# A layer's late work inside a chunked recurrence: late normalisings reordered, VectorE's third step split around the output's normalising, late transposes and one inverse product placed later

## The chip, the cores and the metric

One core of a Trainium2 chip runs the whole program. The metric is the device time in microseconds (us) of one execution; the time shown for a kernel is the median of its runs.

## The reference

Input x has 8 sequences of 1024 tokens with 256 channels, all float32. Six residual blocks follow each other, each on the layer-normed x:

```
x = x + 0.5 * ffn0(LN(x))          # silu(gate) * up, 768 hidden, int weights / 127
x = x + gated_delta_attention(LN(x))  # 16 heads, key 64, value 128, causal conv of 4 taps
x = x + 0.5 * ffn0(LN(x))
x = x + 0.5 * ffn1(LN(x))          # token shift, sigmoid(r) * (relu(k)^2 @ Wv)
x = x + block_attention(LN(x))     # 16 heads of 16, blocks of 64 tokens, rope, softmax
x = x + 0.5 * ffn1(LN(x))
```

The gated delta attention is a recurrence over tokens with a state S of 64 x 128 per head: S = a_t (S - b_t k_t k_t' S) + k_t v_t', o_t = S' q_t, then an RMS norm of o and a product with Wo.

## The kernel before, in words

**Passes.** The tokens are taken in 16 groups of 512 (two per sequence). One pass of the loop handles one group: the first feed-forward block, the projections and convolutions, and then the recurrence in 8 chunks of 64 tokens, written with the inverse of a unit triangular 64 x 64 matrix per head. A pass takes about 450 us here. Everything behind the recurrence (the second half of the layer for the group before: `tail`) is cut into steps and put between the parts of the recurrence, as filler. After the 16th pass the last group's tail runs alone.

**Order by hand.** Every engine has its own instruction stream, and the order in it is written out. Each engine's `tail` is a Python generator; `fill(n)` advances it n times. Ten steps come ahead of chunk 0 (`FILL_FIRST`), then 24 slots (`SLOTS`), three per chunk: slots 3c, 3c+1 and 3c+2 in chunk c (`FILL`). The group's 512 tokens are worked on as two halves of 256, h = 0 and 1, each a stream of 20 late steps; `LATE_AT` says in which slot each step of each half stands. In what follows "step 4 of half 0" is index 4 of that list. The steps on TensorE are: 0 transposes of the normed half (`x{h}s`), 1 token shift products, 2 value product, 3 transposes for the attention (`x{h}a`), 4 query/key/value rows, 5 spread, 6 transposed queries and keys (`kt`), 7 to 10 scores, 10 to 13 weighted values, 14 transposes of the output, 15 output product, 16 transposes for the last feed-forward block (`x{h}u`), 18 shift products, 19 value product. Half 0 has step 2 in slot 2, step 3 in slot 4, and step s in slot s+1 from there on; half 1 has steps 0 and 1 in slots 3 and 4, and step s in slot s+4 from step 2 on.

**VectorE's part of a step** has two pieces, so its streams yield twice per step: in a slot all first pieces run, then all second ones. `values` (lines 602 to 612) adds to x and takes the statistics of the half (`stats`, 493 to 503); GpSimd raises the variance to the power -1/2 (`rstd`, 1092 to 1096); `normal` (505 to 511) waits for that and writes the normed half, for which TensorE's transposes wait (1664). `mix` (582 to 600) makes the two shifted inputs of the last block from ScalarE's copy of the transposes.

**A chunk c on TensorE** (2109 to 2170): wait for the state, product with the old state, slot 3c, transposes of the normalised output of chunk c-2 (two halves through one PSUM bank, bank 2, which ScalarE must copy out before it is written again: `copied`), query product, output of chunk c-1, `solve` (needs `right_side`, line 2032), the rest of the output, slot 3c+1, `new_state`, the projection of a finished part, keys transposed, slot 3c+2. **On VectorE** (978 to 1023): `right_side(c)`, slot 3c, `mean_square(c-1)`, slot 3c+1, `s_update(c)`, `keys(c+1)`, `normalise(c-1)` (934 to 939, it reads what GpSimd made of the mean square), slot 3c+2.

**The inverse in two halves.** GpSimd inverts 32 x 32 cells by substitution (`substitute`, 1169 to 1179), in pieces between its own slots: the second half's substitutions 8 to 15 stand between slots 1 and 2, 16 to 30 in chunk 1. SyncE moves the cells through DRAM, and TensorE and ScalarE make the corner blocks from them with two products: `inverse_q` and `inverse_t`. In chunk 3 the second half's `inverse_q(1,0)` waits for bank 2 (`copied`), then for the cells (`d_back`, 2135 and 2136), and stands ahead of `solve`; `inverse_q(1,1)` stands behind slot 10, `inverse_t` in slot 11 and chunk 4 (waits at 2120 and 2131). ScalarE's copies for them (1450 to 1463) stand in its own stream, some behind an exponential of the softmax (1340 to 1345).

**PSUM ring.** Tail steps use banks 5 to 7 in turn, in the order of `tail_ring`; a step that claims a bank waits (1658) until the step three names ahead of it is read out. The wait instruction that the profile names is the last of several in a row.

## Time and profile before

| What | Value |
| --- | --- |
| Median of 3 runs | 7401.95 us (7399.27 to 7410.97) |
| The profiled execution, its own time | 7407.52 us |
| Its span (first to last instruction) | 7405.7 us, mean granted TensorE clock 0.925 |
| TensorE busy | 85% |
| VectorE, ScalarE, GpSimd busy | 62%, 35%, 31% |
| DMA | mean 31 GB/s, 10.2% of 16 engines |

Times in the timelines are from the start of the span. The pass looked at below is the fifth; its recurrence starts near 2073 us, and the next pass starts near 2286 us. "PEq L2032" as the releaser of a wait of PE means that PE's own sequencer stood at the waiting instruction of line 2032. A row of a timeline may merge instructions; x32 of 64x128 float32 matmuls are 16 matmuls of the source, as float32 goes through the array twice.

### The profile page before, as it was taken

Reading aid. Unit: us, or ns where it says so; the run is one execution under the profiler, and the core shown is the slowest. Engines: PE = TensorE matmul, PEld = TensorE weight load, DVE = VectorE, ACT = ScalarE, POOL = GpSimd, SP = SyncE. Lnnn points to the kernel's source line nnn. Section 1 sums busy time; section 2 is a strip of 40 time slices with the busy share of each in tenths; the row PEclk is TensorE's granted clock in tenths of the full one; section 3 lists DMA queues with packets and bytes.
Section 4 is the critical chain, followed back from the end, with each engine's and each line's share of the span. In section 5 each row is a group of like instructions: output and inputs, shape, how many; then the busy total and the mean of one; then the engine's idle time right before and its main releaser. Section 6 shows DMA issues by size and latency. Waiting matters only on the chain. (4 is left out here: it accounts for less than half of the span.)

```text
span 7405.7 us, 162691 instructions
## 1 busy us (share of the span) xinstructions
PE 6273.3 (85%) x60192; PEld 4534.7 (61%) x60192; DVE 4571.7 (62%) x9685; ACT 2619.0 (35%) x5275; POOL 2269.1 (31%) x3893
## 2 busy tenths in 40 slices
PE   7888888888888888888888889888888888888887
PEld 4665656656576665756656566565756657566575
DVE  6656575565756657566566656657566575665664
ACT  3324243332423325243242433425233252433421
POOL 2513224141331514315133241413315143151421
PEclk9999998999989999999999989899999999999998
DMA  1111001011010101001110010110101110011100
GB/s 53 33 38 22 27 31 39 30 23 40 21 36 30 33 35 29 23 29 33 41 23 27 31 39 30 23 40 21 36 30 33 39 25 23 29 33 41 23 27 5
DMA packets 376536, 226.37 MB, mean 31 GB/s; under 512 B 336896, under 2 KB 353920, under 8 KB 367488
## 3 DMA queue, kind: packets, MB, share of 16 engines
q1 hardware_dynamic: 375680, 215.29, 10.2%
q8 instruction: 496, 8.13, 0.5%
q14 instruction: 360, 2.95, 0.1%
HBM read 156.54 MB, written 58.72 MB: 29 GB/s over the span
## 5 line engine op out<-in xcount | busy, mean ns | idle before, releaser
L833 DVE SCALAR_TENSOR_TENSOR PS<-BIG,CW,PS 128x512 f32<-128x512 f32 x1536 | 1155.2, 753 | 210.2 <-DVEq L831 132.0
L1586 PE MATMUL PS<-BIG 64*64 64x128 f32 (+3 forms) x23200 | 1067.6, 255 | 203.7 <-PEq L2032 105.8
L1586 PEld LDWEIGHTS PS<-BIG 64*64 64x64 f32 (+2 forms) x23200 | 906.7, 134 | 344.8 <-issue 332.9
L1586 PE MATMUL PS<-XT,BIG 128*128 128x512 f32 x2048 | 1058.8, 650 | 51.3 <-PEq L1897 51.3
L1589 PE MATMUL PS<-CST,BIG 128*128 128x128 f32 x3536 | 560.0, 297 | 314.5 <-PEq L1664 82.7
L1589 PEld LDWEIGHTS PS<-CST,BIG 128*128 128x128 f32 x3536 | 416.6, 150 | 434.6 <-issue 417.8
L1249 POOL TENSOR_TENSOR FR<-MS,NHALF 128x8 f32<-128x8 f32 x128 | 209.9, 1640 | 1477.3 <-POOLq L1248 1303.5
L1586 PEld LDWEIGHTS PS<-XT,BIG 128*128 128x128 f32 x2048 | 398.5, 206 | 395.6 <-issue 386.2
L1095 POOL TENSOR_TENSOR RSTD<-VAR,NHALF 128x2 f32<-128x2 f32 x202 | 142.3, 704 | 1574.9 <-POOLq L1094 1568.2
L1586 PE MATMUL PS<-BIG,CST 128*128 128x256 f32 (+1 forms) x1360 | 505.0, 516 | 112.9 <-PEq L1967 98.9
L1177 POOL TENSOR_TENSOR BIG<-BIG 128x30 f32<-128x30 f32 (+14 forms) x960 | 499.9, 521 | 136.5
L1174 POOL TENSOR_TENSOR BIG<-BIG 128x30 f32<-128x30 f32 (+14 forms) x960 | 474.7, 494 | 139.8 <-POOLq L1213 12.0
L1586 PE MATMUL PS<-XT,WG 128*128 128x256 f32 (+1 forms) x1200 | 433.2, 487 | 45.0 <-PEq L1658 20.7
L1586 PE MATMUL PS<-BIG,VO 128*128 128x256 f32 x2080 | 468.3, 382 | 0.9 <-PEq L2216 0.9
L1586 PEld LDWEIGHTS PS<-BIG,CST 128*128 128x128 f32 x1360 | 264.2, 206 | 330.5 <-issue 305.1
L1586 PEld LDWEIGHTS PS<-CST,BIG 64*64 64x64 f32 (+1 forms) x4224 | 328.4, 166 | 191.7 <-issue 189.1
L1586 PEld LDWEIGHTS PS<-BIG,VO 128*128 128x128 f32 x2080 | 394.4, 191 | 66.4 <-issue 14.4
L1586 PE MATMUL PS<-XT,WU 128*128 128x256 f32 (+1 forms) x1200 | 406.5, 462 | 1.0 <-issue 1.0
L964 DVE TENSOR_REDUCE MS<-BIG 128x4 f32<-128x512 f32 x256 | 174.4, 685 | 364.4 <-DVEq L963 364.0
L1421 ACT ACTIVATE BIG<-PS 128x512 f32<-128x512 f32 x512 | 304.2, 594 | 206.4 <-ACTq L1420 206.3
L1586 PE MATMUL PS<-WD,BIG 128*128 128x256 f32 x1584 | 352.5, 381 | 21.9 <-PEq L1632 18.3
L1586 PE MATMUL PS<-CST,BIG 64*64 64x64 f32 (+1 forms) x4224 | 334.1, 235 | 31.9 <-PEq L1864 22.9
(152 smaller groups left out, 10183.3 us busy)
## 6 DMA issues: line engine op xcount, KB each, us to landing
BIG<-in_wv SPq DMA_DIRECT2D x16, 2048.0 KB, 7.5
BIG<-in_wo SPq DMA_DIRECT2D x16, 2048.0 KB, 8.7
BIG<-in_wq SPq DMA_DIRECT2D x16, 1024.0 KB, 4.8
BIG<-in_wk SPq DMA_DIRECT2D x16, 1024.0 KB, 7.3
cells_in<-BIG SPq DMA_DIRECT2D x128, 128.0 KB, 2.7
BIG<-cells_in SPq DMA_DIRECT2D x32, 512.0 KB, 3.8
cells_out<-BIG SPq DMA_DIRECT2D x32, 512.0 KB, 2.6
cells_nat<-BIG SPq DMA_DIRECT2D x32, 512.0 KB, 3.1
```

Of the source, the lines that this page charges most:

```text
L833: op = v.scalar_tensor_tensor(y, pre[:, j:j + G], CW[:, i * TAPS + j:i * TAPS + j + 1], y, ALU.mult, ALU.add)
L964: v.tensor_reduce(MS[:, 4 * x:4 * x + 4], v3(SQO[c][:, 512 * x:512 * x + 512], 4), AX, ALU.add)
L1095: q.tensor_tensor(out=RSTD[:, 2 * k:2 * k + 2], in0=VAR[:, 2 * k:2 * k + 2], in1=NHALF[:, 0:2], op=ALU.pow).then_inc(rstd_ready, 1)
L1174: q.tensor_tensor(out=tmp, in0=each(cells[:, 0:j, j], j, w), in1=over(cells[:, j, j + 1:SUB], j, w), op=ALU.mult)
L1177: q.tensor_tensor(out=cells[:, 0:j, j + 1:SUB], in0=cells[:, 0:j, j + 1:SUB], in1=tmp, op=ALU.add)
L1249: q.tensor_tensor(out=FR[:, :], in0=MS[:, :], in1=NHALF[:, :], op=ALU.pow).then_inc(fr_ready, 1)
L1421: a.activation(TH[:, (i % 2) * G:(i % 2) * G + G], conv_bank(i), ACT.Tanh, scale=0.5).then_inc(cth_ready, 1)
L1586: return nc.tensor.matmul(out_, l, r, start=start, stop=stop)
L1589: return nc.tensor.matmul(out_, in_, ident, is_transpose=True, start=True, stop=True)
```

## The change

- In VectorE's tail each slot now yields once more, behind the first piece of half 0. `fill(2)` is then a whole slot; in slots 3c+2 with c below 7 there is `fill(1)`, `normalise(c-1)`, `fill(1)`: half 0's first piece stands ahead of the normalising, the rest behind it.
- `normal(1)` of slot 2 is put ahead of `values(0)` of that slot (it stood behind it). `normal(0)`, which stood at the end of slot 2, is put into slot 3, behind `mix(1)`.
- The transposes `x{h}u` (TensorE, with ScalarE's copy) move from step 16 to step 17: half 0 from slot 17 to 18, half 1 from slot 20 to 21. VectorE's `mix(h, 1)` moves with them. The ring's order is changed to match.
- In chunk 3, `inverse_q(1,0)` and ScalarE's copy for it move from ahead of `solve(3)` to behind the output of chunk 2, just ahead of slot 10; the wait for the cells and for bank 2 moves with it, and the wait for the copy (`qp_ready`) now stands behind slot 10.

```diff
--- before.py
+++ after.py
@@ -50,7 +50,7 @@
     names.update({5: [f"vd{h}0", f"vd{h}1"], 6: [f"kt{h}0", f"kt{h}1"], 7: [f"sc{h}0"], 8: [f"sc{h}1"]})
     for i in range(5):
         names[9 + i] = ([f"av{h}{i - 1}"] if i else []) + ([f"pt{h}{i}"] if i < 4 else []) + ([f"sc{h}{i + 2}"] if i < 2 else [])
-    names.update({14: [f"oa{h}"], 15: [f"ao{h}"], 16: [f"x{h}u"], 18: [f"k{h}u", f"r{h}u"], 19: [f"v{h}u"]})
+    names.update({14: [f"oa{h}"], 15: [f"ao{h}"], 17: [f"x{h}u"], 18: [f"k{h}u", f"r{h}u"], 19: [f"v{h}u"]})
     return names
 
 
@@ -679,7 +679,8 @@
                     yield
                     values(h, 0)
                     yield
-                    normal(h, x, TXN, txn_ready)
+                    if h == 1:
+                        normal(h, x, TXN, txn_ready)
                     yield
                     yield
                     yield
@@ -730,9 +731,9 @@
                     yield
                     normal(h, x, TXN, txn_ready)
                     yield
+                    yield
+                    yield
                     mix(h, 1)
-                    yield
-                    yield
                     yield
                     yield
                     yield
@@ -758,18 +759,23 @@
                 yield
                 streams = late(0), late(1)
                 for n in range(SLOTS):
-                    now = [streams[h] for h in range(2) if n in LATE_AT[h]]
-                    for s in now:
-                        next(s)
+                    if n == 2:
+                        normal(1, x, TXN, txn_ready)
+                    for h in range(2):
+                        if n in LATE_AT[h]:
+                            next(streams[h])
+                        if h == 0:
+                            yield
                     if n == 0:
                         hidden(1, 4)
                         hidden(1, 5)
                     if n == 1:
                         down(1)
-                    if n == 2:
-                        normal(1, x, TXN, txn_ready)
-                    for s in now:
-                        next(s)
+                    if n == 3:
+                        normal(0, x, TXN, txn_ready)
+                    for h in range(2):
+                        if n in LATE_AT[h]:
+                            next(streams[h])
                     yield
 
             def cp(i):
@@ -987,12 +993,12 @@
                 for c in range(CHUNKS):
                     right_side(c, 0)
                     right_side(c, 1)
-                    fill(FILL[c][0])
+                    fill(2)
                     if c >= 1:
                         mean_square(c - 1)
                     if c == CHUNKS - 1:
                         dve.drain().then_inc(r_free, 1)
-                    fill(FILL[c][1])
+                    fill(2)
                     if c == CHUNKS - 1:
                         break
                     s_update(c, 0)
@@ -1000,10 +1006,11 @@
                     if c >= 5:
                         projected(c - 5, XS[p])
                     keys(c + 1)
+                    fill(1)
                     if c >= 1:
                         normalise(c - 1, 0)
                         normalise(c - 1, 1)
-                    fill(FILL[c][2])
+                    fill(1)
                 last = CHUNKS - 1
                 s_update(last, 0)
                 s_update(last, 1)
@@ -1012,7 +1019,7 @@
                 projected(last - 5, XS[p])
                 input_stats()
                 mean_square(last)
-                fill(FILL[last][2])
+                fill(2)
                 input_normal()
                 xt_copy()
                 normalise(last, 0)
@@ -1392,8 +1399,8 @@
                     act.drain().then_inc(oat_ready, 1)
                     yield
                     yield
+                    yield
                     transposed(f"x{h}u")
-                    yield
                     yield
                     squared(h, 1)
                     yield
@@ -1495,8 +1502,6 @@
                         act.drain().then_inc(a_done, 1)
                     if c >= 2:
                         output(c - 2, 0)
-                    if c == 3:
-                        inverse_q(0, bank(2))
                     for x in range(2):
                         act.wait_ge(u_ps, 1)
                         act.sem_inc(u_ps, -1)
@@ -1507,6 +1512,8 @@
                         output(c - 2, 1)
                     if c >= 1:
                         square_out(c - 1, 1)
+                    if c == 3:
+                        inverse_q(0, bank(2))
                     fill(FILL[c][1])
                     if c == 3:
                         inverse_q(1, bank(2))
@@ -1823,8 +1830,8 @@
                     pe.sem_inc(oat_ready, -1)
                     rows(f"ao{h}", OT, WOUT, KT, ao_ps)
                     yield
+                    yield
                     transposed(f"x{h}u")
-                    yield
                     yield
                     shift(h, 1)
                     yield
@@ -2130,27 +2137,24 @@
                         pe.wait_ge(ti_ready, 1)
                         pe.sem_inc(ti_ready, -1)
                         output_t(c - 2, 0)
+                    solve(c, 0)
+                    solve(c, 1)
+                    if c >= 2:
+                        copied()
+                        output_t(c - 2, 1)
+                    if c >= 1:
+                        output(c - 1, 1)
+                    if c == CHUNKS - 1:
+                        break
                     if c == 3:
                         copied()
                         pe.wait_ge(d_back, 96)
                         pe.sem_inc(d_back, -96)
                         inverse_q(1, 0, bank(2))
-                    solve(c, 0)
-                    solve(c, 1)
-                    if c >= 2:
-                        if c == 3:
-                            pe.wait_ge(qp_ready, 1)
-                            pe.sem_inc(qp_ready, -1)
-                        else:
-                            copied()
-                        output_t(c - 2, 1)
-                    if c >= 1:
-                        output(c - 1, 1)
-                    if c == CHUNKS - 1:
-                        break
                     fill(FILL[c][1])
                     if c == 3:
-                        copied()
+                        pe.wait_ge(qp_ready, 1)
+                        pe.sem_inc(qp_ready, -1)
                         inverse_q(1, 1, bank(2))
                     new_state(c)
                     if c in (2, 4):
```

## Rows read from the trace of the kernel before

**Rows 1.** The page of the kernel before: busy time and share of each engine.

```profile
PE 6273.3 (85%) x60192; PEld 4534.7 (61%) x60192; DVE 4571.7 (62%) x9685; ACT 2619.0 (35%) x5275; POOL 2269.1 (31%) x3893
```

**Rows 2.** Waits of TensorE (PE): whose line, us in total, times, longest.

```profile
PE PS L1586 <- PEq L2032: 105.8, 32, 5.9
...
PE PS L1586 <- PEq L1717: 95.5, 43, 4.4
PE PS L1589 <- PEq L1664: 82.7, 38, 4.4
...
PE PS L1586 <- PEq L2160: 35.2, 16, 2.2
...
PE PS L1586 <- PEq L2136: 31.6, 16, 2.1
```

**Rows 3.** Timeline of TensorE, chunks 0 and 1: start, us, instructions, [idle before].

```profile
2093.37 1.10 PE L1586 MATMUL PS<-S,KQ 64*64 64x128 f32 x32 [0.29 <-PEq L2112]
2098.16 1.09 PE L1589 MATMUL PS<-CST,BIG 128*128 128x128 f32 x4 [3.68 <-PEq L1664]
...
2107.67 5.39 PE L1586 MATMUL PS<-BIG 64*64 64x128 f32 x48 [4.81 <-PEq L2032]
2112.98 0.69 PE L1589 MATMUL PS<-CST,BIG 128*128 128x128 f32 x4
```

**Rows 4.** Timeline of VectorE (DVE), chunks 0 to 2.

```profile
2093.75 0.68 DVE L606 SCALAR_TENSOR_TENSOR BIG<-BIG,PS 128x512 f32<-128x512 f32 x1
...
2096.59 1.43 DVE L510 TENSOR_SCALAR BIG<-XB,MVR,RSTD 128x256 f32<-128x256 f32 x2
2105.12 1.36 DVE L510 TENSOR_SCALAR BIG<-XB,MVR,RSTD 128x256 f32<-128x256 f32 x2 [7.11 <-DVEq L508]
2106.41 2.15 DVE L928 SCALAR_TENSOR_TENSOR BIG<-PS,NBG,VO 128x128 f32<-128x128 f32 x8
...
2134.52 0.73 DVE L510 TENSOR_SCALAR BIG<-XB,MVR,RSTD 128x256 f32<-128x256 f32 x2 [1.04 <-DVEq L508]
```

**Rows 5.** Timeline of GpSimd (POOL), chunks 1 and 2.

```profile
2104.26 0.71 POOL L1095 TENSOR_TENSOR RSTD<-VAR,NHALF 128x2 f32<-128x2 f32 x1 [0.24 <-POOLq L1094]
...
2129.02 2.51 POOL L1105 TENSOR_TENSOR BIG<-BIG 128x512 f32<-128x512 f32 x2 [0.28 <-POOLq L1103]
```

**Rows 6.** Timeline of TensorE, chunks 2 and 3.

```profile
2135.08 2.03 PE L1586 MATMUL PS<-CST,BIG 64*64 64x64 f32 x64
...
2154.72 3.09 PE L1586 MATMUL PS<-BIG 32*32 32x32 f32 x96 [2.14 <-PEq L2136]
...
2159.35 0.66 PE L1589 MATMUL PS<-CST,BIG 128*128 128x128 f32 x4
```

**Rows 7.** Timeline of ScalarE (ACT), chunk 3.

```profile
2153.66 0.60 ACT L1476 ACTIVATE VO<-PS 128x512 f32<-128x512 f32 x1 [0.20 <-ACTq L1474]
```

**Rows 8.** Timeline of SyncE's queue, the last issue of the second scatter.

```profile
2133.60 1.21 SPq L434 DMA_DIRECT2D BIG<-cells_nat  x2
```

**Rows 9.** DMA issues by kind: KB each, median us to landing.

```profile
BIG<-cells_nat SPq DMA_DIRECT2D x64, 128.0 KB, 3.7
```

**Rows 10.** Timeline of VectorE, chunks 3 and 5.

```profile
2173.40 0.69 DVE L644 TENSOR_TENSOR BIG<-PS,CST 128x512 f32<-128x512 f32 x1 [1.87 <-DVEq L643]
...
2229.66 1.28 DVE L938 TENSOR_TENSOR BIG<-PS,FR 128x512 f32<-128x512 f32 x2
...
2233.51 0.28 DVE L668 TENSOR_TENSOR BIG<-PS,NBR 128x128 f32<-128x128 f32 x1
```

**Rows 11.** Timeline of TensorE, chunks 6 and 7.

```profile
2233.99 1.07 PE L1589 MATMUL PS<-CST,BIG 128*128 128x128 f32 x8 [2.88 <-PEq L1816]
...
2263.22 2.12 PE L1586 MATMUL PS<-BIG 64*64 64x128 f32 x32 [1.30 <-PEq L2032]
```

**Rows 12.** Busy time by stretch: PE, PEld, DVE, ACT, POOL, granted clock, DMA.

```profile
2113.00:2152.00 39.00, 38.66 (x504) 29.94 (x504) 29.11 (x72) 10.00 (x17) 23.52 (x35) 1.00 0.21 49
2165.00:2176.00 11.00, 8.65 (x140) 6.15 (x140) 6.47 (x16) 2.74 (x6) 2.34 (x4) 0.69 0.01 2
```

More of the change, by code:

```diff
@@ L732, in late @@
                     yield
-                    mix(h, 1)
                     yield
                     yield
+                    mix(h, 1)
                     yield
```

## The prediction

> **What bounds the kernel now.** I read the page first: TensorE is busy 85% of the span and no other engine is near it [rows 1], so time is won where TensorE stands still, or where its order makes it stand still later. TensorE's waits come next [rows 2]. I looked where they lie in the timelines of several passes: except for the first and last microseconds they come in the same places, with nearly the same length, in all 16 passes, so I work one pass out (the fifth) and multiply by 16. The stretch that the change touches is the recurrence, some 210 of 450 us.
>
> In chunk 1 TensorE waits 3.68 us for normed rows (line 1664) and then 4.81 us for the right side (line 2032) [rows 3]. VectorE shows why: it has finished `normal(1)` late, at 2098.02, and then waits 7.11 us at `normal(0)` before it may start `right_side(1)` at 2106.41 [rows 4]. That wait ends with GpSimd's `rstd(0)` at 2104.26 [rows 5], which stands in GpSimd's queue behind eight substitutions. A small operation of the filler holds up the recurrence through VectorE's in-order queue.
>
> **The parts, one by one.** The unit is one pass; "lead" is how far TensorE is ahead of the trace before.
>
> *Slots 2 and 3.* `normal(1)` now runs at 2093.75 for 1.43 us and `values(0)` with its statistics, 2096.59 - 2093.75 = 2.84 us, behind it [rows 4]. The transposes of slot 3 can start at about 2095.3 instead of 2098.16 [rows 3]. `right_side(1)` starts at about 2098.0 instead of 2106.41, and `solve` follows 1.26 us later (2107.67 - 2106.41) if TensorE is there; it is at about 2100, since the 4.7 us of work between the two waits was done at a low clock. Lead: about 8 us. What is late next is `normal(0)`: VectorE reaches it after `right_side(1)` (2.15 us) and `mix(1)` by about 2104, and must still wait for `rstd(0)`, done at 2104.97; with its 1.36 us it ends at 2106.4, and the transposes of slot 4 start there instead of at 2112.98 [rows 3 to 5]. Lead: 6.5 us; about 3 us if the new 4.6 us wait brings half clock for as long as in this stretch.
>
> That lead is not kept. GpSimd's chain of substitutions does not move (it never waited in this stretch for what gets earlier), so the rope additions behind it still end at 2129.02 + 2.51 = 2131.5 [rows 5]. TensorE's `kt` in slot 7 needs them and starts at 2135.08 now [rows 6]: lead at most 3.5 us. Behind them in GpSimd's queue are `rstd(1)`, the power for the output's norm and the masked keys; passing through `normal(1)`, which already waits 1.04 us [rows 4], they cost about another 1. **I take 2.5 us.** Bounds: 0, if that chain does not move at all; 6.5, if it does not bind.
>
> *`inverse_q(1,0)`.* The wait before it (2136) is named for the cells, but the cells are long there: the last transfer is issued by 2133.60 + 1.21, and such a transfer lands 3.7 us after its issue, at about 2138.5 [rows 8, 9]. What ends the wait at 2154.72 [rows 6] is bank 2: ScalarE's copy of the transposed output runs 2153.66 to 2154.26 [rows 7], behind an exponential that needs VectorE's softmax piece. In the new place `solve`, 4 transposes and the output's second part cover that copy: 32 + 16 matmuls took 5.39 us at half clock, so some 2.7 us at full, and the transposes 0.7 us [rows 3], and the product waits instead for the next copy of bank 2, about 0.9 us, as ScalarE has four passes of 0.6 us [rows 7] to do behind `solve`. So 1.97 us (31.6 / 16 [rows 2]) minus 0.9 and a little for lost overlap: slot 10 starts about 1.6 us earlier. Since the output of chunk 2 is then ready over 3 us earlier, `mean_square(2)`, the softmax piece and ScalarE's second `inverse_q` copy come earlier too, and the 2.20 us wait at 2160 (35.2 / 16) gives back another 0.5. **I take 2.1 us.** Bounds: 0 and 1.97 + 2.20 = 4.2.
>
> *Third step on both sides.* `normalise` takes 1.28 us for both halves [rows 10]. In slot 5 and slot 8 its place changes nothing: the rest of the slot waits for TensorE either way. In slot 11 it did lie in a hole: VectorE did it and then still waited 1.87 us for scores at 2173.40 [rows 10]. Now scaling and the softmax of half 0 come first and the normalising delays half 1's softmax, the exponential and ScalarE's `inverse_t` copy behind it, for which TensorE already waits at 2120: **a loss of 1.0 us** (bounds 0 and 1.28). In slot 14 it is the other way: TensorE waits 4.4 us at scores for a ring bank that `scaled(0,3)` frees (line 1717 [rows 2]; the longest of that row), and that small operation stood behind the normalising. **Gain 1.2 us** (0 to 1.28).
>
> *Transposes one step later.* In slot 17 VectorE does the normalising, then `mix(0,1)`, and only then `scaled(1,3)` at 2233.51 [rows 10], for which TensorE waits 2.88 us until 2233.99 [rows 11]. `mix`, all that lies between the normalising's end at 2230.94 and 2233.51, so 2.6 us, is now in slot 18, where `mean_square` waits for TensorE anyway. **Gain 2.6 us** (0 to 2.88). In slot 20 `mix(1,1)` goes too, but there the normalising now stands behind `values(0,1)`, ends near 2260.8, and chunk 7's transposes of the output need it: TensorE's 1.30 us at `solve` [rows 11] turn into a wait of the same size a little ahead of it. **0 us** (0 to 1.3). The moved transposes and copies are the same instructions; no DMA moves.
>
> *The cost of company.* VectorE's pieces that now run while GpSimd substitutes are slower: `normal` took 1.43 and 1.36 us there and 0.73 us elsewhere [rows 4]. My sum has the long values. The Trainium skill (SBUF — State Buffer, section "SBUF: two separate sides") says that VectorE in a two-port mode, or with two SBUF inputs, and GpSimd lock each other out for a whole instruction. By it more of VectorE's work in slots 2 and 3 would come out slower, but only ahead of `rstd(0)`, where VectorE waits anyway.
>
> Sum: 2.5 + 2.1 - 1.0 + 1.2 + 2.6 = 7.4 us a pass, 16 passes: 118 us. The tail that runs alone at the end has waits of the same kind; I take nothing for it, within 4 us either way. Against the profiled execution: 7407.5 - 118 = 7289; that execution is 5.6 us above the median of the runs, so the median to expect is 7284 us, 1.6% less.
>
> **The rivals.**
>
> *GpSimd keeps all of the first part.* Its chain runs from `rstd(1)` through 24 substitutions to the masked keys with hardly a gap. If it also sets the scores of slot 8, the 2.5 us are gone and 4.9 us a pass stay: 7402 - 78 = 7324. For it: the lead shrinks at every station of that chain. Against: TensorE, not GpSimd, had the last word at `kt` (3.5 us spare). Chance 0.15.
>
> *More comes than I count.* Half clock follows the waits: 0.69 granted in the stretch around 2170 [rows 12]. If shorter waits keep the clock up there and the losses in slot 11 hide, 10 to 11 us a pass: about 7235. Chance 0.12.
>
> *Slower: the clock in chunks 1 to 3.* From 2113 to 2152 TensorE runs at full clock and is busy 38.66 of 39 us [rows 12]. The change puts new short waits into just this stretch (`kt`, scores of slot 8, bank 2) and brings two products of tiny matmuls closer together. At half clock a microsecond of work takes two. If more than 7.4 us of full-clock work in a pass runs at half clock that does not now, the kernel is slower; with 10 us of it, 16 x 2.6 = 42 us slower, 7444. Against: each of the new waits in it is 1 us or less, and TensorE stays busy between them. Chance 0.06.
>
> *It doesn't do what it says.* `normal(0)` still waits for the same power, only one slot later; if every lead is taken back by the next in-order wait, in slots 4, 11 and 21, nothing is left: 7395 to 7402. Chance 0.05.
>
> **How the numbers follow.** My forecast has 0.62. The range 7225 to 7345 leaves out the last two rivals and little else: its lower end is 11 us a pass, its upper end 3.6 us. About 0.2%, 15 us, is what a measurement of this kernel can tell from no change. Faster 0.88 (forecast, the first two rivals, most of the fringe), same 0.05, slower 0.07.
>
> **What would show it.** Right: the 7.11 us wait of VectorE ahead of `right_side(1)` is gone, and a wait of about 1 us stands ahead of `normal(0)` in slot 3; TensorE waits near 4.6 us at line 1664 in slot 4; `kt` starts just behind the rope additions; the waits at d_back and at `scaled(1,3)` are gone; the wait at `inverse_t` grows by about 1 us. Passes last about 443 us. Wrong: the clock below 1.0 between `kt` and slot 9; the wait at 2160 grown; passes at 450.

## The result and the profile after

The changed kernel takes 7283.84 us (median of 4 runs, 7280.8 to 7293.09), the kernel before 7406.46 us: ratio 0.9827 (95% interval 0.9811 to 0.9843). The prediction was 7284 us. So the forecast held, and since a sum can be right with wrong terms, most of what follows is on its terms.

The page of the changed kernel: the span is 125 us shorter. Some 86 us of that are waits of TensorE. The other 39 us are its busy time, for the same 60192 matmuls [rows 1]: it stood 1005 us of this trace at half clock (1.2 GHz granted and not 2.4), and 1115 us of the trace before. The busy times of the other engines are within 10 us of what they were.

```profile
span 7280.3 us, 162691 instructions
...
PE 6234.2 (86%) x60192; PEld 4502.9 (62%) x60192; DVE 4575.7 (63%) x9685; ACT 2616.4 (36%) x5275; POOL 2260.1 (31%) x3893
```

Waits of TensorE, as in [rows 2]. Line 2039 is the old 2032 (right side), 1724 the old 1717 (scores), 1671 the old 1664 (normed rows), 2164 the old 2160 (`qp_ready` behind `new_state`), 2152 the old 2136 (cells and bank 2).

```profile
PE PS L1596 <- PEq L1671: 120.8, 55, 5.5
...
PE PS L1593 <- PEq L1724: 102.6, 68, 3.2
...
PE PS L1593 <- PEq L2164: 30.9, 16, 1.9
...
PE PS L1593 <- PEq L2039: 22.1, 17, 1.4
...
PE PS L1593 <- PEq L2152: 6.6, 16, 0.5
...
PE PS L1596 <- PEq L1823: 3.5, 16, 0.2
```

The wait at the right side fell from 105.8 to 22.1 us, the one ahead of the moved inverse product from 31.6 to 6.6, and `scaled(1,3)` now costs 3.5 us in all (it was 2.88 us in each pass). The wait for normed rows grew from 82.7 to 120.8 us: that is where the stall of chunk 1 went.

Chunks 0 and 1 of the fifth pass. TensorE, VectorE and GpSimd, as in [rows 3 to 5]; this pass starts its recurrence 33.5 us earlier than in the trace before, so 2107.67 there answers to 2074.1 here:

```profile
2065.25 3.00 PE L1593 MATMUL PS<-BIG 64*64 64x128 f32 x48 [1.37 <-PEq L2039]
2073.78 1.09 PE L1596 MATMUL PS<-CST,BIG 128*128 128x128 f32 x4 [5.53 <-PEq L1671]
...
2098.96 2.08 PE L1593 MATMUL PS<-CST,BIG 64*64 64x64 f32 x64 [1.55 <-PEq L1665]
```

```profile
2060.23 0.98 DVE L510 TENSOR_SCALAR BIG<-XB,MVR,RSTD 128x256 f32<-128x256 f32 x2
...
2061.90 0.69 DVE L608 SCALAR_TENSOR_TENSOR XB<-BIG,XB 128x512 f32<-128x512 f32 x1
...
2063.98 2.16 DVE L934 SCALAR_TENSOR_TENSOR BIG<-PS,NBG,VO 128x128 f32<-128x128 f32 x8
...
2072.27 1.36 DVE L510 TENSOR_SCALAR BIG<-XB,MVR,RSTD 128x256 f32<-128x256 f32 x2 [2.39 <-DVEq L508]
```

```profile
2061.91 1.14 POOL L1184 TENSOR_TENSOR BIG<-BIG 128x210 f32<-128x210 f32 x1
...
2066.19 1.08 POOL L1181 TENSOR_TENSOR BIG<-BIG 128x234 f32<-128x234 f32 x1
...
2071.41 0.70 POOL L1102 TENSOR_TENSOR RSTD<-VAR,NHALF 128x2 f32<-128x2 f32 x1 [0.24 <-POOLq L1101]
...
2096.17 2.49 POOL L1112 TENSOR_TENSOR BIG<-BIG 128x512 f32<-128x512 f32 x2 [0.28 <-POOLq L1110]
```

`right_side(1)` starts at 2063.98, 8.9 us earlier in the pass. VectorE reaches `normal(0)` and waits 2.39 us for the power that GpSimd finishes at 2072.1, and the transposes of slot 4 wait 5.53 us for it. `kt` (2098.96) starts when GpSimd's rope additions are done (2096.17 + 2.49); in all 16 passes it starts 0.30 us behind their end.

Chunk 3, as in [rows 6, 7]: the moved product waits 0.49 us for bank 2, behind ScalarE's copy at 2119.75.

```profile
2118.57 0.66 PE L1596 MATMUL PS<-CST,BIG 128*128 128x128 f32 x4
2119.16 1.09 PE L1593 MATMUL PS<-BIG 64*64 64x128 f32 x16
2120.74 1.20 PE L1593 MATMUL PS<-BIG 32*32 32x32 f32 x64 [0.49 <-PEq L2152]
...
2129.51 0.68 PE L1593 MATMUL PS<-CST,KQ 64*64 64x64 f32 x16 [1.90 <-PEq L2164]
```

```profile
2119.27 0.59 ACT L1489 ACTIVATE BIG<-PS 128x512 f32<-128x512 f32 x1
2119.75 0.60 ACT L1483 ACTIVATE VO<-PS 128x512 f32<-128x512 f32 x1
```

To see each part of the sum I took, in every trace, the start of one VectorE operation per chunk, counted from the first `keys` operation of its pass, and the median over the 16 passes (us; for "pass", over 15; the last column is the lead; the names are those of VectorE's functions):

```
mark                before   changed   lead
right_side(1)        33.54     24.62   8.92
s_update(1)          45.01     41.75   3.26
right_side(3)        75.08     73.00   2.08
keys(4)              96.34     92.16   4.18
right_side(4)       106.31    103.48   2.83
right_side(5)       136.28    131.81   4.47
keys(6)             155.92    151.07   4.84
s_update(6)         177.17    168.97   8.20
s_update(7)         196.63    188.30   8.33
pass                449.10    441.18   7.92
```

Medians don't add exactly, and in chunks 3 to 5 a mark carries up to 1 us of noise: `right_side(5)` stands at 136.3 us in the kernel before and at 137.2 us in the one below that changes only slots 17 to 21. On the mean the 15 steps from one pass to the next give 8.2 us each, 123 of the 125 us.

### The profile page after: what moved, and what is told of

Same layout as the page of the kernel before. It is cut to its first block and busy times, and to the rows that moved or that the text cites. A ratio compares the mean times of both kernels' runs of the same rounds, so it can differ in the third digit from the quotient of the medians.

```text
span 7280.3 us, 162691 instructions
## 1 busy us (share of the span) xinstructions
PE 6234.2 (86%) x60192; PEld 4502.9 (62%) x60192; DVE 4575.7 (63%) x9685; ACT 2616.4 (36%) x5275; POOL 2260.1 (31%) x3893
## 5 line engine op out<-in xcount | busy, mean ns | idle before, releaser
L1593 PE MATMUL PS<-BIG 64*64 64x128 f32 (+3 forms) x23200 | 1011.0, 249 | 104.9 <-PEq L2127 36.9
L1593 PEld LDWEIGHTS PS<-BIG 64*64 64x64 f32 (+2 forms) x23200 | 854.6, 130 | 243.8 <-issue 231.9
L1596 PE MATMUL PS<-CST,BIG 128*128 128x128 f32 x3536 | 573.7, 302 | 321.5 <-PEq L1671 120.8
L1315 ACT ACTIVATE XT<-PS 128x512 f32<-128x512 f32 x136 | 82.1, 604 | 805.6 <-ACTq L1314 805.5
```

The lines of the kernel that those rows point to most:

```text
L1315: a.activation(XTH[:, :, h, 1:HG + 1], v3(ps, KT), ACT.Copy).then_inc(free, 1)
L1593: return nc.tensor.matmul(out_, l, r, start=start, stop=stop)
L1596: return nc.tensor.matmul(out_, in_, ident, is_transpose=True, start=True, stop=True)
```

## The experiments

Two theories stood against each other for every part: mine by its sum, and that the part does nothing or the opposite.

**The four parts alone**, each put into the kernel before. The tail's additional `yield` in each slot is in all of them and changes no order by itself; only the third kernel puts something at it.

The order of the normalisings:

```diff
@@ tail of VectorE, the steps, then the slots @@
-                    normal(h, x, TXN, txn_ready)
+                    if h == 1:
+                        normal(h, x, TXN, txn_ready)
...
+                    if n == 2:
+                        normal(1, x, TXN, txn_ready)
                     for h in range(2):
                         if n in LATE_AT[h]:
                             next(streams[h])
...
-                    if n == 2:
-                        normal(1, x, TXN, txn_ready)
+                    if n == 3:
+                        normal(0, x, TXN, txn_ready)
                     for h in range(2):
                         if n in LATE_AT[h]:
                             next(streams[h])
```

> The kernel before with the new order of normal(0) and normal(1) alone. Theory A (the lead of chunk 1 is cut by GpSimd's rope additions, and some of it is kept): 2.1 to 2.5 us a pass are kept at right_side(3), so 34 to 40 us, 7366 us, ratio 0.995; right_side(1) 8 to 9 us earlier, TensorE's wait ahead of the transposes of slot 4 about 5 us. Rival (GpSimd's chain keeps all of it): ratio 1.000. Second rival (nothing binds when ScalarE and bank 2 are left as they were): over 5 us a pass, ratio 0.989.

Measured: 7378.05 us, ratio 0.996 (0.9946 to 0.9974). `right_side(1)` 8.9 us earlier, `s_update(1)` 3.2 us, `right_side(3)` 2.3 us, and `s_update(7)`, near the end of the pass, 1.7 us. TensorE's wait ahead of slot 4's transposes is 5.55 us. A lead of 8.9 us shrinks to a quarter, as in theory A; the ratios of both rivals (1.000 and 0.989) lie outside the interval.

The inverse product:

```diff
@@ TensorE @@
-                    if c == 3:
-                        copied()
-                        pe.wait_ge(d_back, 96)
-                        pe.sem_inc(d_back, -96)
-                        inverse_q(1, 0, bank(2))
                     solve(c, 0)
...
-                    fill(FILL[c][1])
                     if c == 3:
                         copied()
+                        pe.wait_ge(d_back, 96)
+                        pe.sem_inc(d_back, -96)
+                        inverse_q(1, 0, bank(2))
+                    fill(FILL[c][1])
+                    if c == 3:
+                        pe.wait_ge(qp_ready, 1)
+                        pe.sem_inc(qp_ready, -1)
                         inverse_q(1, 1, bank(2))
@@ ScalarE @@
-                    if c == 3:
-                        inverse_q(0, bank(2))
                     for x in range(2):
...
                         square_out(c - 1, 1)
+                    if c == 3:
+                        inverse_q(0, bank(2))
```

> The kernel before with inverse_q(1,0) and its copy moved alone. Theory A (the wait named for the cells is bank 2): the wait of 1.97 us shrinks to 0.5 to 0.9 us and keys(4) comes 2.0 us earlier after right_side(3), 30 to 35 us in all, ratio 0.9955. Rival (the cells are really late): the wait stays as long as the solve lets it, under 1 us a pass, ratio 0.998 to 1.000.

Measured: 7375.28 us, ratio 0.9949 (0.9933 to 0.9966). TensorE in chunk 3 of its sixth pass:

```profile
2580.63 0.63 PE L1592 MATMUL PS<-CST,BIG 128*128 128x128 f32 x4
2581.18 1.09 PE L1589 MATMUL PS<-BIG 64*64 64x128 f32 x16
2582.74 1.20 PE L1589 MATMUL PS<-BIG 32*32 32x32 f32 x64 [0.46 <-PEq L2148]
```

The wait of 1.97 us is 0.46 us, and `keys(4)` comes 2.7 us earlier than in the kernel before. The product itself starts some 1.8 us later in the pass than it did, so this kernel alone can't tell bank 2 from cells that land late. It could have been read off the trace before, where the cells had landed some 14 us before the wait began, that the name of the wait was not its cause. Two other kernels show it: with the normalisings alone the cells land as before (at 65.6 us of the pass, before 65.1) and the product, in its old place, starts 2.3 us earlier; and in the kernel with GpSimd's new order, further down, the cells land 7.3 us later than in the changed kernel, and the moved product starts at 77.4 us of the pass, before the change at 81.2.

The third step on both sides:

```diff
@@ recurrence of VectorE, end of chunk c @@
                     keys(c + 1)
+                    fill(1)
                     if c >= 1:
                         normalise(c - 1, 0)
                         normalise(c - 1, 1)
-                    fill(FILL[c][2])
+                    fill(1)
```

> The kernel before with VectorE's third step on both sides of normalise alone. Theory A (one slot loses what another gains): right_side(4) 1.0 to 1.3 us later, right_side(5) 1.2 to 1.4 us earlier against it, sum 0 within 0.5 us a pass, ratio 0.999 to 1.001. Rival (the split is a gain by itself, as it was in slot 14): 1.2 us a pass, ratio 0.9975.

Measured: 7468.36 us, ratio 1.0076 (1.0059 to 1.0093). Both theories missed: alone, this part makes the kernel 0.8% slower. The marks say where: `right_side(4)` 1.4 us later and `right_side(5)` 1.8 us earlier against it, as expected, and then `s_update(6)` 2.1 us and `s_update(7)` 3.3 us later than before. In slots 17 and 20 `mix` is still there. The split puts it ahead of the normalising in slot 17, and in slot 20 it puts the normalising behind `values(0,1)`, so that others get both late. VectorE in slot 17 of the sixth pass, and TensorE there and in chunk 7:

```profile
2695.06 0.17 DVE L588 COPY XT<-PREV 128x2 f32<-128x2 f32 x1 [0.65 <-DVEq L584]
...
2696.14 1.67 DVE L598 SCALAR_TENSOR_TENSOR BIG<-BIG,MU,XT 128x256 f32<-128x256 f32 x4
2697.73 1.28 DVE L941 TENSOR_TENSOR BIG<-PS,FR 128x512 f32<-128x512 f32 x2
2698.93 0.28 DVE L668 TENSOR_TENSOR BIG<-PS,NBR 128x128 f32<-128x128 f32 x1
```

```profile
2699.40 1.94 PE L1593 MATMUL PS<-CST,BIG 128*128 128x128 f32 x8 [3.62 <-PEq L1820]
...
2728.69 0.63 PE L1593 MATMUL PS<-CST,BIG 128*128 128x128 f32 x4 [1.51 <-PEq L2085]
...
2732.15 2.12 PE L1590 MATMUL PS<-BIG 64*64 64x128 f32 x32 [0.94 <-PEq L2036]
```

`mix` waits 0.65 us for its copy, which the normalising had covered, and `scaled(1,3)` comes behind both: TensorE waits 3.62 us, not 2.88. In chunk 7 it waits 1.51 us for the normalised output and then 0.94 us for the right side, where it had one wait of 1.30 us.

The late transposes and `mix`:

```diff
@@ VectorE @@
                     yield
-                    mix(h, 1)
                     yield
                     yield
+                    mix(h, 1)
                     yield
@@ ScalarE, and the same on TensorE @@
                     yield
-                    transposed(f"x{h}u")
                     yield
+                    transposed(f"x{h}u")
                     yield
```

> The kernel before with the late transposes and mix one step later alone. Theory A (mix stood ahead of scaled(1,3) and of right_side(7)): slot 17 gives 2.6 to 3.4 us and, as normalise stays ahead of values in slot 20, that slot gives another 1.3 us: 3.9 to 4.7 us a pass, 62 to 75 us, ratio 0.991. Rival (slot 20 gives nothing, as in the changed kernel): 2.6 to 3.4 us a pass, ratio 0.9935.

Measured: 7328.41 us, ratio 0.9892 (0.9873 to 0.9911), 83 us and the largest part. Slot 17's wait is 0.22 us, `right_side(7)` starts 5.6 us earlier. The interval holds theory A's 0.991 and not the rival's 0.9935; the gain is a little above A's 62 to 75 us. Slot 20 does give its part here: from `s_update(6)` to `s_update(7)` this kernel takes 17.8 us, the one before 19.5 us.

**The last two together**, as their effects alone were of opposite sign:

```diff
                     keys(c + 1)
+                    fill(1)
...
-                    mix(h, 1)
                     yield
                     yield
+                    mix(h, 1)
```

> The kernel before with two parts together: the third step on both sides of normalise, and the late transposes and mix one step later. Alone they gave 1.0076 and 0.9892. Theory A (what the split costs alone in slots 17 and 20 is mix, which it leaves behind the normalising there, so it costs little once mix is gone): ratio 0.989 to 0.991. Rival (the effects add): ratio 0.997.

Measured: 7360.25 us, ratio 0.9925 (0.9908 to 0.9941). Nearer to theory A, though beyond its 0.991, and clear of the 0.997 of plain addition. Against the late step alone the split costs some 0.3%, though the two intervals just touch (0.9911 and 0.9908). Over the ratios of the parts, -0.0040 (normals), -0.0051 (inverse) and -0.0075 (these two) make -0.0166, and the whole change measured -0.0173: apart from the pair, the parts add.

**What cuts the first lead.** Two edits of GpSimd's order in the changed kernel. First, its power for `normal(0)` moved between the substitutions:

```diff
@@ recurrence of GpSimd @@
                     fill(FILL[c][1])
-                    if c < 2:
-                        substitute(8 + 15 * c, 16 + 15 * c)
+                    if c == 0:
+                        substitute(8, 12)
                     if c == 1:
+                        substitute(23, 31)
                         finish_cells()
                     fill(FILL[c][2])
+                    if c == 0:
+                        substitute(12, 16)
```

> The changed kernel with GpSimd's rstd(0) of slot 2 put between substitutions 11 and 12 instead of behind 15. Theory A (what cuts the lead is the end of GpSimd's whole chain at the rope additions): the wait ahead of the transposes of slot 4 falls from 5.5 to 3 us or less, but right_side(3) comes at the same 73.0 us of the pass within 0.5 us, ratio to before 0.982 to 0.984. Rival (the wait in slot 4 and the clock behind it set the lead): right_side(3) 2 to 3 us earlier, ratio 0.977.

Measured: 7304.82 us, ratio 0.9858 (0.9831 to 0.9884). That is some 20 us above the changed kernel, but the two intervals overlap (0.9811 to 0.9843 there), so the times alone don't show it slower; the marks go against both theories: `right_side(3)` comes at 74.4 us of the pass, 1.4 us later than in the changed kernel. TensorE, VectorE and GpSimd around `kt` in its sixth pass:

```profile
2549.33 3.58 PE L1596 MATMUL PS<-CST,BIG 64*64 64x64 f32 x64 [3.78 <-PEq L1668]
```

```profile
2549.84 0.73 DVE L510 TENSOR_SCALAR BIG<-XB,MVR,RSTD 128x256 f32<-128x256 f32 x2 [6.94 <-DVEq L508]
```

```profile
2546.55 2.48 POOL L1112 TENSOR_TENSOR BIG<-BIG 128x512 f32<-128x512 f32 x2 [0.28 <-POOLq L1110]
2548.98 0.71 POOL L1102 TENSOR_TENSOR RSTD<-VAR,NHALF 128x2 f32<-128x2 f32 x1
```

The last of these stretches, by busy time and granted clock (columns as in [rows 12]), and below it the same 64 matmuls in the changed kernel:

```profile
2549.30:2552.80 3.50, 3.47 (x64) 3.41 (x64) 2.09 (x5) 0.60 (x1) 1.01 (x2) 0.53 1.20 188
```

```profile
2098.90:2101.00 2.10, 2.04 (x65) 2.00 (x65) 1.53 (x4) 0.60 (x1) 0.42 (x1) 1.00 0.94 149
```

`s_update(1)` came 2.7 us earlier still. But the rope additions end where they ended, TensorE waits 3.78 us at `kt` instead of 1.55, and the granted clock is 0.53 behind it, the level of 1.2 GHz, where the changed kernel has 1.00: the 64 matmuls take 3.58 us and not 2.08. From `right_side(2)` to `s_update(3)` the changed kernel has no half clock in any of its 16 passes, this one has a stretch in 14 (the kernel before in 4, of 3.4 us each). In those 14 passes TensorE had waited 3.4 to 5.1 us at `kt`; in the other two it had waited 2.4 and 2.5 us, and the 64 matmuls took 2.08 us. In the changed kernel the longest of these waits is 1.55 us, and in 12 of the 16 passes it is 0.86 us or less. `s_update(2)` is 1.7 us later than in the changed kernel. Arriving earlier at a fixed gate cost time.

Second, the rope additions ahead of the last four substitutions as well:

```diff
@@ recurrence of GpSimd, with the edit above @@
                     if c == 1:
-                        substitute(23, 31)
-                        finish_cells()
+                        substitute(23, 27)
                     fill(FILL[c][2])
...
+                    if c == 1:
+                        substitute(27, 31)
+                        finish_cells()
```

> The changed kernel with GpSimd's rstd(0) put between substitutions 11 and 12, and its rope additions of slot 5 ahead of the last four substitutions. Theory A (GpSimd's chain is what cuts the lead): kt of slot 7 starts 3 us or more earlier, right_side(3) 2.5 to 4 us earlier than in the changed kernel, ratio to before 0.974 to 0.977. Rival (the lead is then lost at the next station, masked keys or the cells of the second half, which now come 2.5 us later): ratio 0.981 or more.

Measured: 7295.94 us, ratio 0.9835 (0.9803 to 0.9868): the rival, though at a station that it didn't name. `kt` starts 3.7 us earlier in its pass than in the changed kernel (median), `right_side(3)` 0.4 us later, and between them the next transposes wait 3.25 us for `normal(1)`, whose power is now the operation behind the cells' copy:

```profile
2529.25 2.03 PE L1598 MATMUL PS<-CST,BIG 64*64 64x64 f32 x64
2534.54 0.63 PE L1601 MATMUL PS<-CST,BIG 128*128 128x128 f32 x4 [3.25 <-PEq L1676]
```

```profile
2530.58 1.94 POOL L1190 COPY BIG<-BIG 128x1024 f32<-128x1024 f32 x1 [0.17 <-issue]
2532.80 0.71 POOL L1102 TENSOR_TENSOR RSTD<-VAR,NHALF 128x2 f32<-128x2 f32 x1 [0.28 <-POOLq L1101]
```

So the gate is not one operation: each small one behind the substitutions is a gate of its own. All of them moved ahead, and the cells' end some 7 us later in the pass:

```diff
@@ recurrence of GpSimd, on top of the two edits above @@
                         substitute(1 + 15 * c, 8 + 15 * c)
+                    if c == 2:
+                        substitute(28, 31)
...
                     if c == 1:
-                        substitute(23, 27)
+                        substitute(23, 26)
+                    if c == 2:
+                        finish_cells()
                     fill(FILL[c][2])
...
                     if c == 1:
-                        substitute(27, 31)
-                        finish_cells()
+                        substitute(26, 28)
```

> The changed kernel with GpSimd's small late operations of slots 2, 5, 6 and 7 (two powers, the rope additions, the power for the output and the first masked keys) all put ahead of substitutions and of the cells' copy, which end some 7 us later in the pass. Theory A (the lead of chunk 1 is lost at the end of GpSimd's chain, station after station, and the cells have about 13 us to spare): right_side(3) 3 to 4 us earlier than in the changed kernel (69 to 70 us of the pass), kt near 56 us and no wait over 1 us behind it, ratio to before 0.973 to 0.976. Rival (the lead is lost to ScalarE and bank 2 in chunk 3, or the cells are now late): right_side(3) early, but keys(4) no more than 1 us earlier than 92.2 us, ratio 0.980 or more.

Measured: 7224.16 us, ratio 0.9753 (0.9733 to 0.9774). The changed kernel ran again beside it:

> The changed kernel as it is, beside the two below on the same chip. Both theories: ratio to the kernel before 0.981 to 0.984, passes of 441 us.

Measured: 7278.53 us, ratio 0.9828 (0.9808 to 0.9848). In the kernel with GpSimd's new order `right_side(3)` comes at 69.3 us of the pass, in this one at 73.1, and `keys(4)` at 88.3 and 92.3: the lead passes through chunk 3 whole. Theory A, in size too.

**What the split costs in the changed kernel.** Without it:

```diff
@@ recurrence of VectorE, changed kernel @@
                     keys(c + 1)
-                    fill(1)
                     if c >= 1:
                         normalise(c - 1, 0)
                         normalise(c - 1, 1)
-                    fill(1)
+                    fill(2)
```

> The changed kernel with normalise again ahead of the whole third slot. Theory A (the split gives 1.2 to 1.6 us in slot 14 and takes 1.3 us in slot 11 and 1.2 to 1.4 us in slot 20): 1.0 to 1.4 us a pass faster than the changed kernel, 16 to 22 us, ratio to the kernel before 0.980. Rival (the split carries part of the change's gain): slower than the changed kernel, ratio 0.985 or more.

Measured: 7250.25 us, ratio 0.977 (0.974 to 0.9799). With the split left out in chunks 3 and 6 alone:

```diff
-                    fill(1)
+                    if c not in (3, 6):
+                        fill(1)
                     if c >= 1:
                         normalise(c - 1, 0)
                         normalise(c - 1, 1)
-                    fill(1)
+                    fill(2 if c in (3, 6) else 1)
```

> The changed kernel with normalise ahead of the whole third slot in chunks 3 and 6 alone. Theory A: both losses of the split go and slot 14's gain stays: 2.6 us a pass faster than the changed kernel, 40 us, ratio to before 0.977. Rival (TensorE is held at the same places by others, as ScalarE's copies and the masked keys): under 1 us a pass, ratio 0.981 or more.

Measured: 7244.48 us, ratio 0.9773 (0.9746 to 0.98). Both beat the changed kernel; they can't be told apart by their times. The second gains what was expected (40 us; 34 to 39 against the two medians of the changed kernel), the first more than its 16 to 22 us (28 to 34). By the marks, without any split `right_side(4)` is 1.1 us earlier than in the changed kernel and `right_side(5)` 1.6 us later; with the split in place in slot 14 both are earlier, 1.3 and 0.8 us, and `s_update(7)` is 1.95 us earlier.

**Both together**, the best kernel of the study:

```diff
+                    if c not in (3, 6):
+                        fill(1)
...
-                        substitute(8 + 15 * c, 16 + 15 * c)
+                        substitute(8, 12)
...
+                        substitute(28, 31)
```

> The same, with normalise ahead of the whole third slot in chunks 3 and 6 too. Theory A: the two gains lie in different chunks and add: 5.5 to 6.5 us a pass faster than the changed kernel, ratio to before 0.968 to 0.971. Rival (they don't add, as the passes are held elsewhere): no faster than the kernel with the chunks' change alone, 0.976 or more.

Measured: 7171.75 us, ratio 0.9688 (0.9663 to 0.9713). TensorE and GpSimd in chunks 1 and 2 of its sixth pass (the first `keys` of this pass stands at 2448.23):

```profile
2504.07 2.03 PE L1602 MATMUL PS<-CST,BIG 64*64 64x64 f32 x64
2506.03 0.66 PE L1605 MATMUL PS<-CST,BIG 128*128 128x128 f32 x4
```

```profile
2497.30 2.51 POOL L1113 TENSOR_TENSOR BIG<-BIG 128x512 f32<-128x512 f32 x2 [0.24 <-POOLq L1111]
...
2502.59 0.71 POOL L1103 TENSOR_TENSOR RSTD<-VAR,NHALF 128x2 f32<-128x2 f32 x1 [0.24 <-POOLq L1102]
...
2506.22 1.65 POOL L1259 TENSOR_TENSOR FR<-MS,NHALF 128x8 f32<-128x8 f32 x1 [0.45 <-POOLq L1258]
2507.84 2.34 POOL L1122 TENSOR_TENSOR BIG<-BIG,CST 128x256 f32<-128x256 f32 x4
...
2510.44 1.96 POOL L1191 COPY BIG<-BIG 128x1024 f32<-128x1024 f32 x1 [0.17 <-issue]
```

`kt` (2504.07) and the transposes behind it start without a wait: the rope additions are done at 2499.8 and the power for `normal(1)` at 2503.3. The cells' copy (2510.44) is now the last of the group. GpSimd's order brings 54 us (7278.53 - 7224.16, the kernel without the two chunks' edit), and the two chunks 52 us on top of it (7224.16 - 7171.75), more than the 34 to 39 us that they bring in the changed kernel. Together that is 6.7 us a pass, where 5.5 to 6.5 were expected.

## Why the prediction was right, and where not

- **What bounds, and the sum.** Right: TensorE's share stayed and its waits shrank. 7.9 us a pass were gained where 7.4 were summed, and that it is so near is in part luck: slots 2 and 3 and slot 11 came out 0.75 us worse than their terms, slots 14 and 17 some 1.2 us better. The sum is one of waits, but 39 of the 125 us are busy time, that is clock. Most of that lies in chunks 0 and 1, where the gate at `kt` turns it into waiting again; in slot 17 it counts. There the passes aren't alike either: the clock fell in 9 passes of the kernel before and not in 7.
- **Slots 2 and 3, 2.5 us.** Measured: 2.1 at `right_side(3)` in the changed kernel, 2.3 alone. Its course was right, and its sizes partly: the wait ahead of slot 4's transposes is 5.53 us where I had 4.6, and half clock followed (the transposes took 1.09 us; the same at full clock take 0.66). VectorE's wait ahead of `normal(0)` was 2.39 us where about 1 us was said. `normal(0)` ended at 2073.6, which is 2107.1 in the time of the trace before; I had 2106.4. I had taken GpSimd's chain as fixed, and this power came 0.66 us later in every pass. Of the sizes behind it two were wrong and cancelled. The 3.5 us that TensorE had to spare at `kt` were read in the fifth pass, where they are 3.55; over the 16 passes of that trace they are 2.3 to 3.9 with a median of 2.7, and as `kt` starts 0.3 us behind the additions, the lead there is 2.4 us. The further loss up to `right_side(3)` was 0.3 us and not about 1. That GpSimd's chain takes the lead back was a statement of the trace's order alone; the kernels that move its small operations show it, and show that it holds at three stations one behind the other: the power for `normal(0)`, the rope additions, the power for `normal(1)`.
- **The inverse product, 2.1 us.** Measured: from 2.08 to 4.18 us of lead, 2.1. The wait for bank 2 ahead of it was 0.49 us, not 0.9, and the one at the old line 2160 gave back 0.3 us (35.2 to 30.9 us in 16 passes), not 0.5.
- **Slot 11, a loss of 1.0 us.** Measured: 4.18 to 2.83, 1.35 us. Right in its course on VectorE, where `normalise` (2138.78) now stands between two softmax pieces and all of its 1.28 us falls on the path. Wrong in where TensorE would feel it: the wait at `inverse_t` was to grow by about 1 us and did not (line 2127, the old 2120: 36.9 us, before 37.4); a new wait of 1.99 us stands ahead of it, at the scores (line 1724), which claim a ring bank. VectorE and TensorE in the changed kernel:

```profile
2131.89 0.29 DVE L668 TENSOR_TENSOR BIG<-PS,NBR 128x128 f32<-128x128 f32 x1
2134.84 0.69 DVE L644 TENSOR_TENSOR BIG<-PS,CST 128x512 f32<-128x512 f32 x1 [2.66 <-DVEq L643]
...
2138.78 1.29 DVE L944 TENSOR_TENSOR BIG<-PS,FR 128x512 f32<-128x512 f32 x2 [0.19 <-DVEq L943]
2139.99 0.68 DVE L644 TENSOR_TENSOR BIG<-PS,CST 128x512 f32<-128x512 f32 x1
```

```profile
2140.96 1.42 PE L1593 MATMUL PS<-KQ,BIG 64*64 64x256 f32 x8 [1.99 <-PEq L1724]
...
2144.49 1.92 PE L1593 MATMUL PS<-BIG 32*32 32x32 f32 x64 [2.11 <-PEq L2127]
```

- **Slot 14, 1.2 us.** Measured: 2.83 to 4.47, 1.6 us. TensorE's wait at the scores fell from 4.37 to 3.18 us, by 1.2. From `s_update(4)` to `right_side(5)` every kernel without the split in slot 14 takes 10.12 to 10.15 us (means over 16 passes), and every kernel with it 8.6 to 8.8, so the split gives 1.3 to 1.5 us there; why more than the wait is not settled, and the last tenths of the 1.6 are within the noise of the mark.
- **Slot 17, 2.6 us.** The wait gave 2.66 us (2.88 to 0.22). The mark behind it, `s_update(6)`, is 3.4 us further ahead than `keys(6)`, and the rest is clock: between the two the 7 passes of the kernel before without half clock take 20.55 us and the 9 that have some (3.4 us of it in most) take 22.2, while all 16 of the changed kernel take 17.89 with none. 20.55 - 17.89 is the wait, and in 9 of 16 passes some 1.6 us more come with it. This is the term that was most too small: the wait was priced right, and the clock behind it at nothing.
- **Slot 20, 0 us.** Right, as worked out: a wait for the normalised output of 1.36 us takes the place of the 1.30 us at `solve`.

```profile
2219.03 0.63 PE L1596 MATMUL PS<-CST,BIG 128*128 128x128 f32 x4 [1.36 <-PEq L2088]
```

The step that failed on its reasons is the part on the split as a whole. I had it at plus 0.2 us in sum, gain and loss in two slots, and it costs: 0.8% alone, 0.3% with `mix` out of the way, and the changed kernel is faster without it. Slots 17 and 20 were costed with both edits in place, so that the split's loss in slot 20 was hidden in the zero there: from `s_update(6)` to `s_update(7)` the kernel before takes 19.5 us, the late step alone 17.8 us, and the changed kernel 19.3 us, so the split costs 1.5 us there. The slower rival, the clock in chunks 1 to 3, did not come: the clock stayed at full in the changed kernel between `kt` and slot 9. It did come in the kernel that moved one power alone. The rival that more would come, by the clock, was right in kind and wrong in place: from `keys(4)` to `right_side(4)`, the stretch it named, both traces have 75 us of half clock in 16 passes, and what went away was in chunks 0 and 1, in 4 passes of chunk 3, and in slot 17. Of the rival on GpSimd, the part that was true is inside the 2.5 us.

What stays open: why slot 14 gave more than its wait, and which of several small differences makes the clock fall in some passes and not in others behind the same wait of 2.88 us.

## What to carry to other kernels

A stall that is taken away moves its engine up to the next gate, and with in-order queues that gate is often one queue's whole chain: walk the lead from station to station before you count it, and if several small operations stand behind long ones, move all of them or none. Cost an edit once alone and once with the others: here one of four parts was a loss that its neighbours hid. Look at the clock behind a wait as well as at the wait. The name of a wait is that of the last instruction in the queue, so check when each thing it waits for was there.

## What the runs showed of the hardware

- Arriving earlier at a gate that doesn't move can cost time. With a wait of 3.78 us ahead of them, the 64 matmuls of `kt` took 3.58 us (granted clock 0.53), and 2.08 us behind a wait of 1.55 us (granted clock 1.00). In the kernel that moved one power the clock is at half behind this wait in 14 passes of 16.
- VectorE and GpSimd slow each other both ways. `normal` beside the substitutions took 0.98 and 1.36 us in the changed kernel against 0.73 us elsewhere [rows 4]. The substitution at 2061.91 took 1.14 us; it started just behind VectorE's addition to x at 2061.90 (two inputs in SBUF, 0.69 us), and the same substitution in the kernel before, which met the statistics instead, took 0.58. So it lost 0.56 us, where the other's operation had 0.68 us to run. The Trainium skill (SBUF — State Buffer, section "SBUF: two separate sides") has it as a lock, between a VectorE operation with two inputs in SBUF and a GpSimd operation that reads SBUF, that the first to start holds for its whole instruction. This pair agrees with that to about 0.1 us. A second one, at 2066.19, started just behind VectorE's next operation with two inputs in SBUF and took 1.08 us, before 0.60. The kernel before had one such pair there (0.98 us, in the changed kernel 0.56), so the new order costs GpSimd 0.56 + 0.48 - 0.42 = 0.62 us up to the power for `normal(0)`, which ends 0.66 us later in every pass. By the end of the rope additions 0.1 us of it is left (59.0 us of the pass before, 59.1 after, means over 16 passes), so it cost little. Of VectorE's own longer operations, `normal(1)` (0.98 us) was shorter than before (1.43 us), and `normal(0)` (1.36 us) delays slot 4's transposes, but not `kt`, which waits for GpSimd.
